# Experts' second matrix read by TensorE where it lies, through a register, instead of from a copy

## The chip, the cores and the metric

The kernel runs on one core of one Trainium2 chip. The metric is the device time of one execution in microseconds; the median of several runs counts. All data are float32 (indices are integers). The engines are TensorE (PE in the profile), VectorE (DVE), ScalarE (ACT), GpSimd (POOL) and SyncE (SP, which issues most of the transfers). Each works through its own program, and semaphores tie them together.

## The reference

x has 16 rows of 256 tokens of 128 numbers. Four blocks are added to it one after the other: a linear attention, a mixture-of-experts block, a second attention, and the same mixture-of-experts block again. The part that matters here is inside the block that runs twice:

```
logits = xf @ Wg.T
idx = jnp.argmax(logits, axis=-1)
for e in range(E):
    m = (idx == e)[:, None].astype(xf.dtype)
    h = jax.nn.relu(xf @ W1[e] + b1[e])
    out = out + m * (h @ W2[e] + b2[e])
z = _layer_norm(y + _moe(y, Wg, W1, b1, W2, b2), g2, be2)
```

There are 8 experts, W1[e] is 128x512 and W2[e] is 512x128. Each token goes through one expert.

## The kernel before

The 4096 tokens lie in DRAM sorted by expert, each expert's rows padded to whole tiles of 128. There are at most `ET` = 39 tiles, and a table `owner`, built by DVE in `table` shortly before, says for each tile which expert owns it. `experts(n, target)` runs for n = 0 and n = 1, once per mixture block; the two are called the two expert stages. All weights of the experts lie in SBUF for the whole kernel, in `we`: for each expert 512 columns of W1, then 512 of W2 and 128 more that carry the second bias and the residual (`EW` = 1152 columns). The scratch tile `late`, in three slots, is `we_t` in this stage.

Per tile i the engines do this:

- SP loads the tile's rows into `zs` (line 1238, one of nine slots).
- PE transposes them into the bank TB (1250). ACT copies the result to `zt` (1285, semaphore `zt`).
- ACT reads the tile's owner with a value load (1292) and copies the first matrix of that expert, 512 columns, from `we` to `we_t` (1293, semaphore `w1`). DVE reads the owner too (1305) and copies the other 640 columns (1334, semaphore `w2`).
- PE forms the hidden layer in four products (1260). The first two finish `hid_a`, which ACT turns into `hid_e` with a relu (1288, `relu_a`); the last two finish `hid_b`, DVE's share of the relu (1312, `relu_b`).
- PE forms the output in five products, four from `hid_e` (1271) and one from `zt` (1273), in one of three banks (`v`).
- DVE takes the statistics (1308, 1315, 1322), POOL the root (`rstd`, 1219), DVE finishes the layer norm (1318, 1329), and POOL writes the rows to their tokens in DRAM with an indirect transfer (1223).

A float32 product of 128x128 by 128x128 runs in two passes, each with its own weight load (PEld in the profile), so line 1260 has 8 passes per tile and lines 1271 and 1273 have 10.

The order on each engine is written out by hand. Every engine has a function `body(i, s, has, lap)` that holds step i of a software pipeline: `has(k)` says that the part that works on tile i - k is in it. `pipeline` (45) writes the first `first` steps out one by one, puts the rest into a loop of `unroll` steps, and writes the last steps out. PE and DVE have 12 steps written out and a loop of nine that runs three times, ACT has six and a loop of three. In PE's step i the order is: the transpose of tile i, the hidden layer of tile i - 1, the output of tile i - 2. In ACT's: `zt` of tile i, relu of tile i - 1, then owner and first matrix of tile i. In DVE's: owner of tile i, statistics of i - 3, relu of i - 1, the rest of the norm, and at the end the copy for tile i:

```
if has(0):
    after(dve, g["v"], o + i - 2)
    nc.vector.tensor_copy(we_t[:, c, F:], we[:, bass.ds(e, 1), F:].rearrange("p a n -> p (a n)"))\
        .then_inc(g["w2"], 1)
```

PE waits for `w1` ahead of line 1260 and for `w2` ahead of line 1271.
Of the kernel before, what the change touches and what calls it, by code (L numbers as in the profile page):

```python
# [29 lines left out]
P = 128  # L30
# [3 lines left out]
NT = T // P  # L34
# [4 lines left out]
F = 512  # L39
FC = F // P  # L40
E = 8
ET = (T + E * (P - 1)) // P
EW = F + F + D
# [29 lines left out]
def after(eng, sem, count):  # L73

    if not (isinstance(count, int) and count <= 0):
        eng.wait_ge(sem, count)

def build(nc, A, out):

    ctx = ExitStack()
    with ctx:
# [58 lines left out]
        we = sb("we", [P, E, EW])  # L141
# [7 lines left out]
        stats = sb("stats", [P, 3, 6, 6])  # L149
# [7 lines left out]
        zt = sb("zt", [P, 3, 2, 2 * P])  # L157
# [23 lines left out]
        owner = sb("owner", [P, ET], I32)  # L181
# [10 lines left out]
        late = sb("late", [P, 6144])  # L192
# [4 lines left out]
        def parts(whole, *shapes):  # L197

            at, cut = 0, []
            for shape in shapes:  # L200
                size = int(np.prod(shape))
                part = whole[:, at:at + size]
                names = "abcdef"[:len(shape)]
                if len(shape) > 1:
                    part = part.rearrange(f"p ({' '.join(names)}) -> p {' '.join(names)}",
                                          **dict(zip(names[1:], shape[1:])))
                cut.append(part)
                at += size
            assert at <= whole.shape[1], at
            return cut  # L210
# [15 lines left out]

        k_x, p_t = parts(early, (3, 2, 4, HM, 32), (3, 2, HM, P))

        we_t, over, owner_m, skip_m, ends_m = parts(late, (3, EW), (E, NT), (ET, E), (ET, E), (E, E))
        pay, zs = parts(rows_e, (3, 2, PAY), (ZS, PAY))  # L230
        hid_e, = parts(hid_f, (3, FC, P))

# [892 lines left out]
        def table(n):  # L1125
# [61 lines left out]

        e_s = {k: sem("e_" + k) for k in (
            "turned", "zt", "w1", "w2", "hid_a", "hid_b", "relu_a", "relu_b", "v", "stats", "agg", "var",  # L1190
            "rstd", "tmp", "dest", "y")}
        loaded = [sem(f"e_loaded{k}") for k in range(ZS)]
        stored = [sem(f"e_stored{k}") for k in range(3)]
# [5 lines left out]
        def experts(n, target):  # L1199

            o = n * ET
# [39 lines left out]
            def _(pe):  # L1242
                g = e_s

                def body(i, s, has, lap):
# [5 lines left out]
                    if has(1):  # L1251
# [11 lines left out]
                                last.then_inc(g["hid_a"], 1)  # L1263
                        last.then_inc(g["hid_b"], 1)
                    if has(2):
                        pe.wait_ge(g["relu_a"], o + i - 1)
                        pe.wait_ge(g["relu_b"], o + i - 1)
                        pe.wait_ge(g["w2"], o + i - 1)
                        after(pe, g["tmp"], o + i - 4)
                        for m in range(FC):  # L1270
                            nc.tensor.matmul(VB[c2][:, 0:P], hid_e[:, c2, m, :], we_t[:, c2, F + m * P:F + (m + 1) * P],  # L1271
                                             start=(m == 0), stop=False)
                        nc.tensor.matmul(VB[c2][:, 0:P], zt[:, c2, 0, 0:P], we_t[:, c2, 2 * F:], start=False,
                                         stop=True).then_inc(g["v"], 1)
                pipeline(pe, ET, 3, ZS, body, FIRST)

            @on("scalar")
# [21 lines left out]
            def _(dve):  # L1299
                g = e_s  # L1300

                def body(i, s, has, lap):
                    c, c1 = s % 3, (s - 1) % 3
                    if has(0):
                        e = dve.value_load(owner[0:1, bass.ds(i, 1)], min_val=0, max_val=E - 1)
                    if has(3):
                        dve.wait_ge(g["v"], o + i - 2)
                        nc.vector.bn_stats(stats[:, c, 0, :], VB[c][:, 0:P]).then_inc(g["stats"], 1)
# [14 lines left out]
                    if has(4):  # L1323
                        dve.wait_ge(g["tmp"], o + i - 3)
                        if has(7):
# [3 lines left out]
                        nc.vector.scalar_tensor_tensor(out=xout[:, c1, 0, :], in0=tmp[:, c1, 0, :],  # L1329
                                                       scalar=rstd[:, c1, 0:1], in1=row[:, D:2 * D], op0=ALU.mult,  # L1330
                                                       op1=ALU.add).then_inc(g["y"], 1)
                    if has(0):
                        after(dve, g["v"], o + i - 2)
                        nc.vector.tensor_copy(we_t[:, c, F:], we[:, bass.ds(e, 1), F:].rearrange("p a n -> p (a n)"))\
                            .then_inc(g["w2"], 1)
                dve.wait_ge(tabled, n * 2 + 1)
                pipeline(dve, ET, 5, ZS, body, FIRST)

# [226 lines left out]
```

## Time and profile before

| | |
|---|---|
| Median of 3 runs | 846.76 us (845.48 to 848.72) |
| The profiled execution: its own time | 845.9 us |
| The profiled execution: span of its instructions | 844.0 us |
| Mean granted clock of TensorE | 0.908 of full speed |
| Busy: PE, weight loads | 687.7 us (81%), 579.5 us (69%) |
| Busy: DVE, ACT, POOL | 547.8 us (65%), 338.1 us (40%), 476.0 us (56%) |

Busy time counts work on the engine; register operations, waits and the issue of transfers are not in it. The profile's span runs from the first to the last instruction; the execution's own time has 1.9 us more around it. The expert stages lie at about 336 to 436 us and at about 741 us to the end. In the rows further down, "ACT late L1293" is ACT's instruction of line 1293 that writes the tile `late`; a q behind an engine's name (ACTq, DVEq, and PEldq for PE) stands for that engine's sequencer.

### The profile page before, as it was taken

The page shows a single profiled execution, that of the slowest core. Times are in us where ns is not written, and L with a number is a line of the kernel's source. Part 1 is how long each engine was busy: PE and PEld are TensorE (multiplying, and loading weights), DVE is VectorE, ACT ScalarE, POOL GpSimd, SP SyncE. Part 2 cuts the span into 40 slices and gives each one's busy share as a digit, 9 for nine tenths or more (in the row PEclk, how much of TensorE's full clock was granted, in tenths as well). Part 3 has the DMA queues.
Part 4 walks back from the last instruction along what each step waited for, and adds up shares of the span by engine and source line. Part 5 has one row for each costly group of instructions (what it writes and reads, how often), then busy time and mean ns, then how long its engine had stood idle before and what let it go on. Part 6 is the DMA issues. An engine that isn't in the chain of part 4 may idle for free.

```text
span 844.0 us, 18577 instructions
## 1 busy us (share of the span) xinstructions
PE 687.7 (81%) x5238; PEld 579.5 (69%) x5238; DVE 547.8 (65%) x1972; ACT 338.1 (40%) x839; POOL 476.0 (56%) x1098
## 2 busy tenths in 40 slices
PE   5799999877888754999969999995788876089994
PEld 3588888734666653999955877774566755079994
DVE  3788887556999854688842333323489985248885
ACT  2332323125777510555532121220677762045552
POOL 5465656643688870388764233322348887127886
PEclk9999999979999857899988999998799995579997
DMA  7900000040011134233230000004001111423320
GB/s 225 291 13 15 12 19 13 26 106 2 13 39 37 45 126 87 73 86 93 72 108 18 20 13 19 19 14 118 1 2 38 46 42 45 82 73 87 93 84 31
DMA packets 54887, 49.50 MB, mean 59 GB/s; under 512 B 5768, under 2 KB 49743, under 8 KB 54704
## 3 DMA queue, kind: packets, MB, share of 16 engines
q1 hardware_dynamic: 46426, 33.51, 14.8%
q0 software_dynamic: 5568, 13.54, 4.5%
q10 hardware_dynamic: 2838, 1.78, 1.1%
q8 instruction: 26, 0.43, 0.2%
q14 instruction: 29, 0.24, 0.1%
HBM read 31.07 MB, written 19.85 MB: 60 GB/s over the span
## 4 chain that ended last, share of the span: by engine, by line
PE 45%; DVE 23%; POOL 9%; issue 8%; DMA 6%; ACT 4%; DVEq 1%; SPq 1%; ACTq 1%; POOLq 1%
PE bank L1260 7%; PE wide L1397 7%; PE bank L1386 7%; PE wide L1271 4%; DVE early L1029 4%; DVE early L736 3%; POOL rstd L534 3%; DVE stats L511 2%; PE bank L1271 2%; PE wide L456 2%; DVE z L538 2%; DMA sorted_dram<-sorted_dram 2%; POOL sorted_dram L1114 1%; PE wide L871 1%; DMA sorted_dram<-rows_e,pos 1%
## 5 line engine op out<-in xcount | busy, mean ns | idle before, releaser
L520 POOL TENSOR_TENSOR both_m<-stats 128x2 f32<-128x2 f32 (+1 forms) x94 | 19.1, 203 | 175.1 <-DVE stats L511 174.7
L1219 POOL TENSOR_TENSOR rstd<-var_e,half_neg 128x1 f32<-128x1 f32 x78 | 59.0, 756 | 84.3 <-DVE var_e L1322 79.4
L1260 PE MATMUL bank<-zt,late 128*128 128x128 f32 x624 | 90.9, 291 | 1.6 <-issue 1.2
L534 POOL TENSOR_TENSOR rstd<-spread_m,half_neg 128x2 f32<-128x2 f32 (+1 forms) x94 | 86.0, 915 | 7.4
L1260 PEld LDWEIGHTS bank<-zt,late 128*128 128x128 f32 x624 | 78.8, 198 | 8.3 <-issue 4.0
L1114 POOL DMA_INDIRECT sorted_dram<-rows_e,pos x64 | 66.7, 1043 | 15.5 <-issue 14.7
L1312 DVE TENSOR_SCALAR hid_f<-bank 128x256 f32<-128x256 f32 x78 | 33.1, 425 | 49.6 <-PE bank L1260 44.9
L1386 PE MATMUL bank<-late,qk_t 128*128 128x128 f32 x512 | 62.1, 275 | 0.0
L1293 ACT ACTIVATE late<-we 128x512 f32 x78 | 49.2, 631 | 28.6 <-PE bank L1260 24.4
L1397 PE MATMUL wide<-vo,gram 128*128 128x512 f32 x128 | 60.0, 612 | 0.7 <-ACT gram L1444 0.7
L1386 PEld LDWEIGHTS bank<-late,qk_t 128*128 128x128 f32 x512 | 59.6, 192 | 0.0
L1029 DVE STREAM_TRANSPOSE early<-sc 32x256 f32<-32x256 f32 x128 | 55.8, 436 | 1.5
L1271 PE MATMUL wide<-late,hid_f 128*128 128x128 f32 x416 | 55.1, 275 | 0.0
L1464 DVE COPY late<-wide 128x1024 f32<-128x1024 f32 x16 | 19.6, 1225 | 48.0 <-PE wide L1397 48.0
L1271 PEld LDWEIGHTS wide<-late,hid_f 128*128 128x128 f32 x416 | 50.6, 192 | 0.1
L1285 ACT ACTIVATE zt<-bank 128x128 f32<-128x128 f32 x78 | 21.6, 276 | 72.7 <-PE bank L1250 72.7
L1250 PE MATMUL bank<-ident,rows_e 128*128 128x128 f32 x78 | 22.4, 287 | 34.4 <-DMA rows_e<-sorted_dram 34.4
L959 ACT ACTIVATE early<-bank 32x256 f32<-32x256 f32 x128 | 47.4, 371 | 1.1
L1223 POOL DMA_INDIRECT out<-xout,dest x39 | 40.3, 1033 | 6.0 <-issue 5.5
L1223 POOL DMA_INDIRECT x_dram<-xout,dest x39 | 40.3, 1034 | 5.2 <-issue 4.8
L1397 PEld LDWEIGHTS wide<-vo,gram 128*128 128x128 f32 x128 | 23.9, 197 | 25.6 <-issue 24.3
L1288 ACT ACTIVATE hid_f<-bank 128x256 f32<-128x256 f32 x78 | 29.9, 383 | 25.5 <-PE bank L1260 25.5
(247 smaller groups left out, 1878.9 us busy)
## 6 DMA issues: line engine op xcount, KB each, us to landing
rows_e<-sorted_dram SPq DMA_DIRECT2D x78, 128.5 KB
xa<-x_dram SPq DMA_DIRECT2D x9, 640.0 KB, 6.4
we<-L_ffn_W SPq DMA_DIRECT2D x16, 256.0 KB
x_dram<-xout SPq DMA_DIRECT2D x32, 128.0 KB, 1.8
rows_e<-L_ffn_b SPq DMA_DIRECT2D x1, 2048.0 KB
xa<-L_attn_a_x SPq DMA_DIRECT2D x3, 512.0 KB, 6.1
sorted_dram<-sorted_dram ACTq DMA_DIRECT2D x8, 128.5 KB, 6.4
sorted_dram<-sorted_dram SPq DMA_DIRECT2D x8, 128.5 KB, 6.8
```

Source lines behind the costliest of these rows:

```text
L534: nc.gpsimd.tensor_tensor(rstd[:, slot, w], spread_m[:, slot, 0, w], half_neg[:, w], ALU.pow).then_inc(rstd_made, 1)
L959: last = nc.scalar.activation(k_x[rows, c1, :, :, h, :].rearrange("p t q k -> p (t q) k"), QK[rows, 256:512].rearrange("p (n k) -> p n k", ...
L1029: last = nc.vector.transpose(p_t[rows, c3, :, :, 32 * q:32 * q + 32].rearrange("p t h k -> p (t h) k"), sc[rows, c3, :, :, :].rearrange("p ...
L1114: nc.gpsimd.indirect_dma_start(sorted_dram[n][:, :], bass.IndirectOffsetOnAxis(ap=pos[:, c, t:t + 1], axis=0), pay[:, c, t, :], None).then ...
L1219: nc.gpsimd.tensor_tensor(rstd[:, s % 3, 0:1], var_e[:, s % 3, :], half_neg[:, 0:1], ALU.pow).then_inc(g["rstd"], 1)
L1223: nc.gpsimd.indirect_dma_start(target, bass.IndirectOffsetOnAxis(ap=dest[:, c, :], axis=0), xout[:, c, 0, :], None).then_inc(stored[(s - 5 ...
L1260: last = nc.tensor.matmul(to[:, (m % 2) * P:(m % 2 + 1) * P], we_t[:, c1, m * P:(m + 1) * P], zt[:, c1, 0, 0:P], start=True, stop=True)
L1271: nc.tensor.matmul(VB[c2][:, 0:P], hid_e[:, c2, m, :], we_t[:, c2, F + m * P:F + (m + 1) * P], start=(m == 0), stop=False)
L1293: nc.scalar.activation(we_t[:, c, 0:F], we[:, bass.ds(e, 1), 0:F].rearrange("p a n -> p (a n)"), ACT.Copy).then_inc(g["w1"], 1)
L1312: nc.vector.tensor_scalar_max(hid_e[:, c1, 2:4, :], HB_[:, 0:256].rearrange("p (m t) -> p m t", m=2), 0.0).then_inc(g["relu_b"], 1)
L1386: last = nc.tensor.matmul(MB[:, 0:P], qk_t[:, h, :], u_sb[:, c, h * D:(h + 1) * D], start=(h == 0), stop=(h == HB - 1))
L1397: last = nc.tensor.matmul(wide[:, 512 * k:512 * (k + 1)], gram[:, c2, :], vo[:, 4 * k:4 * k + 4, :].rearrange("p h d -> p (h d)"), start=T ...
```

## The change

DVE no longer reads the owner and no longer copies the second matrix; the semaphore `w2` and PE's wait for it are gone. `we_t` shrinks to the 512 columns of the first matrix. PE reads the owner of tile i - 2 itself, behind line 1260 and ahead of the output's products, and these take their second operand from `we` at an address from a register. DVE's wait for the table at the start of the stage moves to PE. ACT's part stays.

```diff
--- before.py
+++ after.py
@@ -226,7 +226,7 @@
 
         k_x, p_t = parts(early, (3, 2, 4, HM, 32), (3, 2, HM, P))
 
-        we_t, over, owner_m, skip_m, ends_m = parts(late, (3, EW), (E, NT), (ET, E), (ET, E), (E, E))
+        we_t, over, owner_m, skip_m, ends_m = parts(late, (3, F), (E, NT), (ET, E), (ET, E), (E, E))
         pay, zs = parts(rows_e, (3, 2, PAY), (ZS, PAY))
         hid_e, = parts(hid_f, (3, FC, P))
 
@@ -1187,7 +1187,7 @@
 
 
         e_s = {k: sem("e_" + k) for k in (
-            "turned", "zt", "w1", "w2", "hid_a", "hid_b", "relu_a", "relu_b", "v", "stats", "agg", "var",
+            "turned", "zt", "w1", "hid_a", "hid_b", "relu_a", "relu_b", "v", "stats", "agg", "var",
             "rstd", "tmp", "dest", "y")}
         loaded = [sem(f"e_loaded{k}") for k in range(ZS)]
         stored = [sem(f"e_stored{k}") for k in range(3)]
@@ -1263,15 +1263,17 @@
                                 last.then_inc(g["hid_a"], 1)
                         last.then_inc(g["hid_b"], 1)
                     if has(2):
+                        e = pe.value_load(owner[0:1, bass.ds(i - 2, 1)], min_val=0, max_val=E - 1)
+                        second = we[:, bass.ds(e, 1), F:].rearrange("p a n -> p (a n)")
                         pe.wait_ge(g["relu_a"], o + i - 1)
                         pe.wait_ge(g["relu_b"], o + i - 1)
-                        pe.wait_ge(g["w2"], o + i - 1)
                         after(pe, g["tmp"], o + i - 4)
                         for m in range(FC):
-                            nc.tensor.matmul(VB[c2][:, 0:P], hid_e[:, c2, m, :], we_t[:, c2, F + m * P:F + (m + 1) * P],
+                            nc.tensor.matmul(VB[c2][:, 0:P], hid_e[:, c2, m, :], second[:, m * P:(m + 1) * P],
                                              start=(m == 0), stop=False)
-                        nc.tensor.matmul(VB[c2][:, 0:P], zt[:, c2, 0, 0:P], we_t[:, c2, 2 * F:], start=False,
+                        nc.tensor.matmul(VB[c2][:, 0:P], zt[:, c2, 0, 0:P], second[:, F:], start=False,
                                          stop=True).then_inc(g["v"], 1)
+                pe.wait_ge(tabled, n * 2 + 1)
                 pipeline(pe, ET, 3, ZS, body, FIRST)
 
             @on("scalar")
@@ -1301,8 +1303,6 @@
 
                 def body(i, s, has, lap):
                     c, c1 = s % 3, (s - 1) % 3
-                    if has(0):
-                        e = dve.value_load(owner[0:1, bass.ds(i, 1)], min_val=0, max_val=E - 1)
                     if has(3):
                         dve.wait_ge(g["v"], o + i - 2)
                         nc.vector.bn_stats(stats[:, c, 0, :], VB[c][:, 0:P]).then_inc(g["stats"], 1)
@@ -1329,11 +1329,6 @@
                         nc.vector.scalar_tensor_tensor(out=xout[:, c1, 0, :], in0=tmp[:, c1, 0, :],
                                                        scalar=rstd[:, c1, 0:1], in1=row[:, D:2 * D], op0=ALU.mult,
                                                        op1=ALU.add).then_inc(g["y"], 1)
-                    if has(0):
-                        after(dve, g["v"], o + i - 2)
-                        nc.vector.tensor_copy(we_t[:, c, F:], we[:, bass.ds(e, 1), F:].rearrange("p a n -> p (a n)"))\
-                            .then_inc(g["w2"], 1)
-                dve.wait_ge(tabled, n * 2 + 1)
                 pipeline(dve, ET, 5, ZS, body, FIRST)
```

Two places show the change in the order of instructions. The first is PE, a tile inside the loop; the names are the tiles and banks written and read, and the semaphores waited for stand in brackets. Before:

```order
L1260 MATMUL bank<-zt,late 128x128 [waits e_relu_a,e_w1,e_zt]
L1260 MATMUL bank<-zt,late 128x128
L1260 MATMUL bank<-zt,late 128x128 [waits e_relu_b]
L1260 MATMUL bank<-zt,late 128x128
L76 REGISTER_ALU [waits e_w2,e_relu_b,e_relu_a]
L1271 MATMUL bank<-late,hid_f 128x128 [waits e_tmp]
L1271 MATMUL bank<-late,hid_f 128x128 x3
L1273 MATMUL bank<-late,zt 128x128
L76 REGISTER_ALU [waits e_loaded6]
```

And now (line 1266 is the value load, 1272 and 1274 are the former 1271 and 1273):

```order
L1260 MATMUL bank<-zt,late 128x128 [waits e_relu_a,e_w1,e_zt]
L1260 MATMUL bank<-zt,late 128x128
L1260 MATMUL bank<-zt,late 128x128 [waits e_relu_b]
L1260 MATMUL bank<-zt,late 128x128
L1266 ISA
L1266 TENSOR_LOAD owner
L1266 ISA x2
L1272 ISA [waits e_tmp,e_relu_b,e_relu_a]
L1272 MATMUL wide<-we,hid_f 128x128
L1272 ISA
L1272 MATMUL wide<-we,hid_f 128x128
L1272 ISA
```

A load and three register operations stand between line 1260 and the output's first product, and one register operation (ISA) ahead of each of the products, of which the last two follow in the same way. Of the three waits of L76, that for `e_w2` is gone.

The second place is DVE, one tile of the loop, before:

```order
L1305 TENSOR_LOAD owner
L1305 ISA x2
L1308 BN_STATS stats<-wide 128x6 [waits e_v]
L1312 TENSOR_SCALAR hid_f<-bank 128x256 [waits e_hid_b,e_stats]
L1315 BN_AGGR mv<-stats 128x2
L1318 SCALAR_TENSOR_TENSOR tmp<-bank,mv,g2f 128x128 [waits e_rstd]
L1322 TENSOR_SCALAR var_e<-mv 128x1 [waits e_agg]
L1328 COPY dest<-rows_e 128x1 [waits e_stored0,e_tmp]
L1329 SCALAR_TENSOR_TENSOR xout<-tmp,rstd,rows_e 128x128
L1334 ISA [waits e_v]
L1334 COPY late<-we 128x640
```

And now:

```order
L1308 BN_STATS stats<-wide 128x6 [waits e_v]
L1312 TENSOR_SCALAR hid_f<-bank 128x256 [waits e_hid_b,e_stats]
L1315 BN_AGGR mv<-stats 128x2
L1318 SCALAR_TENSOR_TENSOR tmp<-wide,mv,g2f 128x128 [waits e_rstd]
L1322 TENSOR_SCALAR var_e<-mv 128x1 [waits e_agg]
L1328 COPY dest<-rows_e 128x1 [waits e_stored1,e_tmp]
L1329 SCALAR_TENSOR_TENSOR xout<-tmp,rstd,rows_e 128x128
```

The load at the head and the copy at the end are gone; the seven instructions between them keep their order and their waits.

## Rows read from the trace of the kernel before

**Rows 1.** The page, the chain that ended last: shares of the span by line.

```profile
PE bank L1260 7%; PE wide L1397 7%; PE bank L1386 7%; PE wide L1271 4%; DVE early L1029 4%; DVE early L736 3%; POOL rstd L534 3%; DVE stats L511 2%; PE bank L1271 2%; PE wide L456 2%; DVE z L538 2%; DMA sorted_dram<-sorted_dram 2%; POOL sorted_dram L1114 1%; PE wide L871 1%; DMA sorted_dram<-rows_e,pos 1%
```

**Rows 2.** Windows over tiles 6 to 37 of the first expert stage.

```profile
core 0: us, PE busy (x) PEld busy (x) DVE busy (x) ACT busy (x) POOL busy (x), PEclk, DMA share, GB/s
352.90:424.00 71.10, 71.10 (x609) 68.63 (x607) 61.01 (x256) 41.32 (x96) 56.76 (x64) 1.00 0.30 84
```

**Rows 3.** The chain in order of time: start us, us, engine and line, passes.

```profile
344.56 0.89 PE bank L1260 x8
...
346.68 0.89 PE bank L1260 x8
...
353.04 1.01 PE bank L1260 x8
...
357.51 0.94 PE bank L1260 x8
...
359.68 1.01 PE bank L1260 x8
...
424.15 1.05 PE bank L1260 x8
```

**Rows 4.** Timeline, loop tiles: start us, us, engine line operation out<-in, count, [idle before].

```profile
380.32 0.38 ACT L1288 ACTIVATE hid_f<-bank 128x256 f32<-128x256 f32 x1 [0.28 <-PE bank L1260]
...
381.10 0.63 ACT L1293 ACTIVATE late<-we 128x512 f32 x1 [0.39 <-PE bank L1260]
...
381.80 0.97 PEld L1260 LDWEIGHTS bank<-zt,late 128*128 128x128 f32 x8
...
382.55 0.38 ACT L1288 ACTIVATE hid_f<-bank 128x256 f32<-128x256 f32 x1 [0.28 <-PE bank L1260]
382.68 0.97 PEld L1271 LDWEIGHTS bank<-late,hid_f 128*128 128x128 f32 x8
...
383.11 0.42 DVE L1312 TENSOR_SCALAR hid_f<-bank 128x256 f32<-128x256 f32 x1
383.26 0.63 ACT L1293 ACTIVATE late<-we 128x512 f32 x1 [0.33 <-issue]
```

**Rows 5.** PE's sequencer (PEldq) in narrow windows: duration ns min/median/max, first and last start.

```profile
L76 PEldq EVENT_SEMAPHORE  x1: 1029/1029/1029, 380.7 to 380.7; - x1
...
L1268 PEldq EVENT_SEMAPHORE  x1: 51/51/51, 381.8 to 381.8; - x1
...
L76 PEldq EVENT_SEMAPHORE  x1: 51/51/51, 381.9 to 381.9; - x1
...
L65 PEldq ALU_OP  x1: 32/32/32, 382.1 to 382.1; - x1
```

**Rows 6.** Waits of the first stage's steady part: total us, times, longest.

```profile
ACT late L1293 <- PE bank L1260: 10.7, 28, 0.4
POOL rstd L1219 <- DVE var_e L1322: 10.0, 27, 0.6
```

**Rows 7.** DVE's value load (L1305, both stages) and copy (L1334, first stage), by source line.

```profile
L1305 DVEq FUSED_REGOPS  x126: 57/190/206, 326.4 to 828.5; - x126
L1305 DVEq TENSOR_LOAD <-owner x78: 299/306/554, 325.8 to 828.1; - x78
...
L1334 DVE COPY late<-we x32: 483/485/495, 353.0 to 422.1; 128x640 f32 x32
```

**Rows 8.** ACT's value load and copy of one tile, by source line.

```profile
L1292 ACTq FUSED_REGOPS  x2: 43/98/152, 380.4 to 380.8; - x2
L1292 ACTq TENSOR_LOAD <-owner x1: 275/275/275, 380.5 to 380.5; - x1
L1292 ACTq SEQ_ASSERT  x1: 18/18/18, 381.0 to 381.0; - x1
...
L1293 ACTq FUSED_REGOPS  x1: 46/46/46, 381.0 to 381.0; - x1
```

**Rows 9.** The page, DMA queues: packets, MB, share of 16 engines.

```profile
q8 instruction: 26, 0.43, 0.2%
```

## The prediction

> **What bounds the kernel now.** I began with the page's chain that ended last: L1260, the experts' first product, stands at its head with 7%, and L1271, the second, is near it [rows 1]. The change lies in the two expert stages, so next came the windows over their steady part (tiles 6 to 37): PE is busy in every microsecond of it, DVE 61 of 71 us, ACT 41, and the granted clock is 1.00, which is the 2.4 GHz level [rows 2]. A full PE looks like a PE bound. The chain in order of time corrects that: in the first tiles L1260 comes every 2.12 us and takes 0.89, from 353 on it comes every 2.16 to 2.24 us (357.51 to 359.68 is one tile, 353.04 to 357.51 are two) and is stretched to 0.93 to 1.01, with the same eight passes [rows 3]. From 353.04 to 424.15 there are 32 tiles, 2.22 us each. So PE loses about 0.1 us in each of 33 tiles per stage, just ahead of L1260, which the page hides in its busy time.
>
> The timeline of one tile shows for what. ACT's copy of the first matrix (L1293) runs from 381.10 to 381.73, and L1260 loads its first weights at 381.80 [rows 4]; PE's sequencer sat in the wait of that moment for 1029 ns from 380.7 [rows 5]. In the next tile the copy ends at 383.89. Thus the bound is a ring: L1260 starts (381.80), its first half gives relu_a on ACT (382.55), ACT reads the owner and forms the address, copies (383.26 to 383.89), and L1260 may start again. **DVE is not in that ring.** The waits of the stretch hold none of PE for DVE's w2: the longest are POOL for DVE's var_e and ACT for L1260 [rows 6].
>
> **The change part by part.** *Taken from DVE:* 78 copies of 128x640 at 485 ns (38 us) and 78 value loads, in which the sequencer spends 306 + 190 ns and more [rows 7]. Who profits? PE asked for w2 two tiles late, so not PE. stats (L1308) could start up to 0.5 us earlier, since it stands behind the copy of 0.49, but bn_aggr, var and POOL's rstd come after relu_b (383.11), which waits for L1260 [rows 4, 6]. I cost the relief at 0; what hides it is that relu_b is tied to PE. If POOL were the last (57 of 71 us busy [rows 2]) it would gain at most those few tenths at a stage's end, once per stage. The wait for w2 falls from PE too; its operation of 51 ns stays in part, since two waits remain.
>
> *Added on PE:* per tile a TENSOR_LOAD, a register operation behind it and an assert, in loop tiles one more register operation for the table's address, and five register operations, one ahead of each of the five products (ten passes). None is array work, all of it is the sequencer's. It does run ahead of the array: it was at the loop's end (L65, 382.1) while L1260's passes of 381.80 to 382.68 were still running, ahead of all of L1271 [rows 4, 5]. But it can't run ahead over the wait for w1, which holds it until 381.77. After that the array is fed until L1271's slot at 382.68, so there are 0.91 us in which the new operations must be through. What do they need? The same value load on ACT takes 43 (address) + 275 + 152 + 18 ns, and 46 more for the copy's address, from 380.4 to the copy's start at 381.10: 0.70 us, so some 30 ns lie between two of them [rows 4, 8]. On PE two operations of 51 ns start at 381.84 and 381.95 (rows from windows of 0.02 us) and the next at 382.1, a good 0.1 apart, so the gaps there are nearer 58 ns [rows 5]. From the gate: 0.075 until the first operation (381.77 to 381.84), 0.101 + 0.336 + 0.210 + 0.076 for the load, 0.109 for the remaining wait, 0.096 for the first address: 1.00 us. In tiles that also form a wait's count (two of the loop's nine) 0.09 more, 1.09. In tiles written out without the loop the table's address falls away: 0.90, in time.
>
> So in the 54 loop tiles L1272 starts 0.09 late, in 12 of these 0.18. PE's own work is 2.12, so it is ready after 2.21 or 2.30, while the ring allows 2.16, 2.23 or 2.24 in turn [rows 3]. Most of the lateness falls into time that PE lost to the ring anyway. I followed it tile by tile: L1272 starts at the later of S + 0.89 and gate + 1.00 (1.09), PE is ready 1.23 later, the next S is the later of that and the ring's; a late S gives the sequencer a lead over the array that shortens the next lateness. 27 tiles come out 0.46 us longer, both stages **+0.9 us**.
>
> Bounds of the two unknown prices. The load: at ACT's 275 ns as above; DVE's median of 306 gives +1.4, and 0.41 us, between that and DVE's worst (554), would give +3.8; a cheaper one than ACT's could save no more than the 0.9 [rows 7, 8]. The register-addressed product: no row of PE has one. Low end: static products, of which the sequencer passes 20 instructions between its wait at 381.9 and the operation at 382.1, next to nothing. High end: each of two passes costs a slot like PE's cheapest operation, 32 + 60 ns, 0.184 per product [rows 5]. The nearest row is ACT's register-addressed copy, which starts at 381.10, directly behind its address operation of 46 ns at 381.0 [rows 4, 8]; I take that, a few hundredths. PE then needs some 0.12 to 0.2 of its sequencer per product, below the array's 0.22 for two passes, and nothing is added; the loss begins at 0.10 extra per product.
>
> The Trainium skill speaks against the change here: "TensorE: Matmul & The Clock Gate", section "Wait — 56ns, not 53.3ns?", says that MATMUL is normally decoded in hardware, and that the sequencer's own code, where it has to do it, spends about 62 ns on each. If a register in the address forces that, by an estimate from this figure the extra is 0.124 per product, the sequencer needs 2.33 us per tile, and the sum would be +6.4 instead of +0.9, 853 us. The trace agrees with hardware decoding for static products (20 in 0.1 us); no row here shows the other.
>
> The head and the tail: the first two tiles are cold and have over 1.6 us between L1260 and L1271; the last product waits for its predecessor, not for its sequencer. 0. **Sum:** 844.0 + 0.9 in the span, with the 1.9 around it 846.8 for the profiled execution. That one ran 0.9 below the median of the runs, 846.76, so I forecast a median of **847.7 us**.
>
> **The rivals.**
> 1. *The sequencer becomes the bound (slower).* Price: from the gate 1.00 + four products' operations 0.50 + the extra + 0.19 for the next tile's wait and transpose + 0.03. It decides from an extra of about 0.10 per product. At the high end (5 x 0.184) that is 2.64 per tile, +0.4 in 54 loop tiles and +0.3 in 18 others, about +28, 875 us; halfway between decision and high end some +14, 861. For it: each operation of PE's sequencer has its 0.1 us, and nothing shows a register-addressed pass there. Against it: ACT's copy. 22%.
> 2. *The load waits for PE's passes to end (slower).* L1260's last pass ends 1.05 after S, the load and what follows take 0.83, so L1272 starts at 1.88 instead of 0.89, +0.9 in 78 tiles: 917 us. Against it: ACT's load begins at 380.5 while its relu_a runs (380.32 to 380.70) [rows 4, 8]. 4%.
> 3. *The loop's code no longer stays in the engine (slower).* PE's loop of nine tiles grows from some 380 instructions (38 passes and weight loads a tile, and some four others) by eight a tile to some 455. A packet of code takes 0.2% of 16 x 844 us over 26 packets, 1.0 us [rows 9]; two of them exposed at each of four back edges is +8, 856 us. 26 packets for the whole run speak against. 3%.
> 4. *The ring isn't the bound and PE is delayed by DVE after all (faster).* Then the 66 tiles fall from 2.22 to 2.12: 66 x 0.10 = -6.8, 840 us. Against it: 0.07 us from the copy's end to L1260 in tile after tile. 5%.
> That the change does less than it says is no case: in the order of instructions the copy and DVE's load are gone, and PE has its own.
>
> **How the numbers follow.** Forecast 66%, from 844.5 to 851 us (load at 0.41, spread of the median). Runs of this kernel tell 0.5% (4.2 us) from no change. Slower: 22 + 4 + 3%, less the mild part of rival 1, plus little of the forecast's own upper end: 29%. Faster: 6%. Within: 65%. The range reaches down to 844.5, which leaves out the 5% of rival 4, and up to 858, which takes in the mild half of rival 1 and rival 3, and leaves out about 15%.
>
> **What would show it.** Right: L1293's end to L1260's start still 0.07 in most tiles, pitch of the loop tiles 2.22 to 2.25, idle or stretch of up to 0.1 ahead of L1272, DVE some 50 us less busy and more idle, POOL unchanged. Rival 1: a pitch of 2.3 or more, L1293 done long before L1260, a stretched L1272. Rival 2: a gap of 1 us ahead of L1272. Rival 3: a gap at the loop's ends alone, and more code packets. Rival 4: 2.12. I am wrong if PE's operations have another price than ACT's.

## The result, and the profile after

| | Before | Changed |
|---|---|---|
| Median, 20 runs each | 847.12 us (844.72 to 850.09) | 848.91 us (846.54 to 852.62) |
| Changed over before | | 1.0026, 95% interval 1.0015 to 1.0037 |
| Profiled execution: own time, span | 845.9 us, 844.0 us | 852.62 us, 850.9 us |

By the ratio the changed kernel takes 2.2 us more of 847 (1.3 to 3.1). It is slower, by less than the 0.5% that the prediction called a difference. The forecast was "within 0.5%", +0.9 us.

The profiled execution of the changed kernel is the slowest of its 20, so its span may not be compared with [rows 1]'s run as a whole. 2.1 us of the 6.9 between the two spans had passed before the first expert product was issued (340.03 against 337.93), where the kernels are the same; 1.5 more lie in the first six tiles of the first stage, which the section on the prediction comes to. The page:

```profile
PE 692.5 (81%) x5238; PEld 585.3 (69%) x5239; DVE 514.2 (60%) x1893; ACT 338.5 (40%) x839; POOL 470.7 (55%) x1098
...
q8 instruction: 28, 0.46, 0.3%
...
PE bank L1260 9%; PE wide L1392 7%; PE bank L1381 7%; PE wide L1272 6%; DVE early L1029 4%; PE bank L1272 3%; DVE early L736 3%; DVE stats L511 2%; POOL rstd L534 2%; DVE z L538 2%; DMA sorted_dram<-sorted_dram 2%; ACT z L974 2%; PE wide L456 2%; DVE sc L1020 1%; DMA sorted_dram<-rows_e,pos 1%
...
L1219 POOL TENSOR_TENSOR rstd<-var_e,half_neg 128x1 f32<-128x1 f32 x78 | 51.1, 655 | 90.5 <-DVE var_e L1322 85.8
...
L1312 DVE TENSOR_SCALAR hid_f<-bank 128x256 f32<-128x256 f32 x78 | 33.1, 425 | 92.6 <-PE bank L1260 59.9
```

DVE lost 33.6 us of busy time (547.8 before), and not a microsecond of it shows in the span: ahead of L1312 it now sits idle for 92.6 us (49.6 before), most of it until PE's L1260 is done. The chain names the same two products as [rows 1], with larger shares. Code packets are 28 instead of 26 [rows 9].

The windows over the 32 tiles from tile 6 to tile 38, first and second expert stage, answer to [rows 2]:

```profile
core 0: us, PE busy (x) PEld busy (x) DVE busy (x) ACT busy (x) POOL busy (x), PEclk, DMA share, GB/s
356.52:429.01 72.49, 72.47 (x609) 70.24 (x608) 47.02 (x225) 41.37 (x96) 54.29 (x65) 1.00 0.29 82
763.70:836.64 72.94, 72.74 (x609) 70.09 (x607) 46.79 (x225) 41.37 (x96) 54.15 (x65) 1.00 0.29 82
```

For the second stage of the kernel before, the same view gives:

```profile
758.53:829.83 71.30, 71.30 (x609) 68.62 (x607) 60.88 (x254) 41.31 (x96) 56.94 (x64) 1.00 0.29 84
```

The first number after the bounds is the length; over 32 it is the pitch of a tile. It was 2.22 us in the first stage and 2.23 in the second, and is 2.27 and 2.28 now, at the same passes and the same granted clock of 1.00. That is +3.0 us over 2 x 32 tiles in this pair of executions, against +2.2 in the timed runs. DVE falls from 61 to 47 us of work in the stretch, ACT stays at 41. PE reads busy throughout in all of these rows, so the busy column tells nothing of the loss. What tells it is the timeline, at the place of [rows 4]:

```profile
380.69 0.63 ACT L1295 ACTIVATE late<-we 128x512 f32 x1 [0.33 <-PE bank L1260]
...
381.47 0.97 PEld L1260 LDWEIGHTS bank<-zt,late 128*128 128x128 f32 x8
...
382.22 0.38 ACT L1290 ACTIVATE hid_f<-bank 128x256 f32<-128x256 f32 x1 [0.17 <-PE bank L1260]
...
382.41 0.97 PEld L1272 LDWEIGHTS wide<-we,hid_f 128*128 128x128 f32 x8
...
383.70 0.97 PEld L1260 LDWEIGHTS bank<-zt,late 128*128 128x128 f32 x8
...
384.87 0.30 PEld L1272 LDWEIGHTS wide<-we,hid_f 128*128 128x128 f32 x2 [0.20 <-issue]
```

Before, L1271 followed L1260 by 0.89 us in every tile. L1272 now follows by 0.94 (381.47 to 382.41) and by 1.17 (383.70 to 384.87), the latter with 0.20 us of empty weight path, released by nobody ("issue"). Over tiles 6 to 38 the mean of this distance is 1.01 us. PE's sequencer shows why, in the first of the two tiles: narrow windows on the wait, the load, the remaining wait and the first address (a q view rounds starts to 0.1):

```profile
L76 PEldq EVENT_SEMAPHORE  x1: 357/357/357, 381.0 to 381.0; - x1
...
L1266 PEldq FUSED_REGOPS  x2: 42/96/151, 381.4 to 381.9; - x2
L1266 PEldq TENSOR_LOAD <-owner x1: 307/307/307, 381.5 to 381.5; - x1
L1266 PEldq SEQ_ASSERT  x1: 18/18/18, 382.1 to 382.1; - x1
...
L76 PEldq EVENT_SEMAPHORE  x1: 51/51/51, 382.2 to 382.2; - x1
...
L1272 PEldq FUSED_REGOPS  x1: 60/60/60, 382.3 to 382.3; - x1
```

The wait for w1 ends at 381.37, 0.05 after ACT's copy (380.69 + 0.63). Then come six operations one after the other, and only at 382.41 the weight load of L1272: 1.04 us after the gate, where 1.00 was forecast. The load is the difference. Over the stretch of the first window its row reads:

```profile
L1266 PEldq FUSED_REGOPS  x59: 42/151/151, 356.9 to 427.4; - x59
L1266 PEldq TENSOR_LOAD <-owner x32: 298/306/417, 356.6 to 427.0; - x32
```

and in the six tiles of it that are written out ahead of the loop:

```profile
L1266 PEldq TENSOR_LOAD <-owner x6: 301/366/417, 356.6 to 368.0; - x6
```

It takes 306 ns in the median, like DVE's, and not 275 like ACT's [rows 7, 8]; the mean over both stages is 317, and nine of the 78 took over 340.

### The profile page after: what moved, and what is told of

It is laid out like the page before. It is cut to its first block, busy times and chain, and to the rows that moved or that the text cites. A ratio compares the mean times of both kernels' runs of the same rounds, so it can differ in the third digit from the quotient of the medians.

```text
span 850.9 us, 18752 instructions
## 1 busy us (share of the span) xinstructions
PE 692.5 (81%) x5238; PEld 585.3 (69%) x5239; DVE 514.2 (60%) x1893; ACT 338.5 (40%) x839; POOL 470.7 (55%) x1098
## 4 chain that ended last, share of the span: by engine, by line
PE 50%; DVE 22%; issue 8%; POOL 7%; DMA 6%; ACT 5%; SPq 1%; ACTq 1%; POOLq 0%; DVEq 0%
PE bank L1260 9%; PE wide L1392 7%; PE bank L1381 7%; PE wide L1272 6%; DVE early L1029 4%; PE bank L1272 3%; DVE early L736 3%; DVE stats L511 2%; POOL rstd L534 2%; DVE z L538 2%; DMA sorted_dram<-sorted_dram 2%; ACT z L974 2%; PE wide L456 2%; DVE sc L1020 1%; DMA sorted_dram<-rows_e,pos 1%
## 5 line engine op out<-in xcount | busy, mean ns | idle before, releaser
L1219 POOL TENSOR_TENSOR rstd<-var_e,half_neg 128x1 f32<-128x1 f32 x78 | 51.1, 655 | 90.5 <-DVE var_e L1322 85.8
L1260 PE MATMUL bank<-zt,late 128*128 128x128 f32 x624 | 89.0, 288 | 1.7 <-issue 1.3
L1312 DVE TENSOR_SCALAR hid_f<-bank 128x256 f32<-128x256 f32 x78 | 33.1, 425 | 92.6 <-PE bank L1260 59.9
L1260 PEld LDWEIGHTS bank<-zt,late 128*128 128x128 f32 x624 | 79.9, 200 | 4.4 <-issue 3.0
L1295 ACT ACTIVATE late<-we 128x512 f32 x78 | 49.2, 631 | 28.4 <-issue 18.5
L1272 PE MATMUL wide<-we,hid_f 128*128 x416 | 58.5, 284 | 0.1
L1272 PEld LDWEIGHTS wide<-we,hid_f 128*128 128x128 f32 x416 | 50.5, 192 | 3.0 <-issue 1.1
L918 PE MATMUL wide<-early,v_r 128*32 128x128 f32 x512 | 22.3, 296 | 21.1 <-DVE early L1029 21.1
```

The source lines that it names most:

```text
L1219: nc.gpsimd.tensor_tensor(rstd[:, s % 3, 0:1], var_e[:, s % 3, :], half_neg[:, 0:1], ALU.pow).then_inc(g["rstd"], 1)
L1260: last = nc.tensor.matmul(to[:, (m % 2) * P:(m % 2 + 1) * P], we_t[:, c1, m * P:(m + 1) * P], zt[:, c1, 0, 0:P], start=True, stop=True)
L1272: nc.tensor.matmul(VB[c2][:, 0:P], hid_e[:, c2, m, :], second[:, m * P:(m + 1) * P], start=(m == 0), stop=False)
L1295: nc.scalar.activation(we_t[:, c, 0:F], we[:, bass.ds(e, 1), 0:F].rearrange("p a n -> p (a n)"), ACT.Copy).then_inc(g["w1"], 1)
L1312: nc.vector.tensor_scalar_max(hid_e[:, c1, 2:4, :], HB_[:, 0:256].rearrange("p (m t) -> p m t", m=2), 0.0).then_inc(g["relu_b"], 1)
```

## The experiments

All are compared with the kernel before on the same chip. "Pitch" is the length of tiles 6 to 38 over 32, first and second stage. "Distance" is the mean time from the first weight load of the hidden layer (L1260) to that of the output (L1271, L1272), and "gate" the median time from the end of ACT's copy to L1260; both are read from the starts and ends in the timeline of the first stage.

| Run | Ratio to before (95%) | Pitch, us | Distance | Gate |
|---|---|---|---|---|
| before | 1 | 2.223, 2.228 | 0.888 | 0.07 |
| changed | 1.0026 (1.0015 to 1.0037) | 2.265, 2.280 | 1.013 | 0.11 |
| e1_early_load | 1.0001 (0.9987 to 1.0014) | 2.230, 2.229 | 0.888 | 0.07 |
| e2_load_only | 1.0013 (0.9998 to 1.0027) | 2.256, 2.263 | 1.006 | 0.08 |
| e3_two_loads | 1.0297 (1.0270 to 1.0325) | 2.608, 2.614 | 1.378 | 0.42 |
| e4_before_act_swap | 0.9950 (0.9932 to 0.9968) | 2.179, 2.189 | 0.952 | 0.40 |
| e5_after_act_swap | 0.9955 (0.9942 to 0.9968) | 2.209, 2.219 | 0.976 | 0.50 |
| e6_early_act_swap | 0.9899 (0.9880 to 0.9918) | 2.142, 2.136 | 0.890 | 0.40 |
| e7_relief_alone | 0.9986 (0.9972 to 1.0000) | 2.223, 2.226 | 0.888 | 0.07 |
| e9_three_loads | 1.0888 (1.0825 to 1.0952) | 3.192, 3.243 | 1.963 | 1.00 |

**Is it the load's place?** e1_early_load is the changed kernel with one edit: PE's load and the address stand at the head of its step, ahead of the transpose and of the wait for w1.

```diff
                     c, c1, c2 = s % 3, (s - 1) % 3, (s - 2) % 3
+                    if has(2):
+                        e = pe.value_load(owner[0:1, bass.ds(i - 2, 1)], min_val=0, max_val=E - 1)
+                        second = we[:, bass.ds(e, 1), F:].rearrange("p a n -> p (a n)")
                     if has(0):
...
                     if has(2):
-                        e = pe.value_load(owner[0:1, bass.ds(i - 2, 1)], min_val=0, max_val=E - 1)
-                        second = we[:, bass.ds(e, 1), F:].rearrange("p a n -> p (a n)")
                         pe.wait_ge(g["relu_a"], o + i - 1)
```

> The changed kernel with PE's value load moved from behind L1260 to the head of the step, ahead of the transpose and of the wait for w1, where PE's sequencer has time to spare. All register addresses and register-addressed products stay. Theory (the load and what follows stand between the w1 gate and the output's first product): the distance from L1260's start to the output's first product falls from 0.95 to 1.1 back to 0.89, the pitch of the gated tiles from 2.27 back to 2.22, and the time to that of the kernel before, 847 us within 1. Rival (the register-addressed products, the longer code, or something outside the expert stages makes the change slower): the time stays 2 us above before, pitch 2.27.

Its time is that of the kernel before, 844.95 against 844.96 us. The windows of both stages:

```profile
354.20:425.57 71.37, 71.35 (x609) 68.78 (x607) 45.54 (x225) 41.30 (x96) 54.39 (x65) 1.00 0.29 83
758.24:829.58 71.34, 71.34 (x609) 68.79 (x608) 45.58 (x225) 41.30 (x96) 54.25 (x65) 1.00 0.28 83
```

71.37 and 71.34 stand beside 71.15 and 71.30 before: all but 0.3 of the 3.0 us is gone, though every added instruction is still there. Ahead of the gate the load runs while PE's sequencer would wait anyway. The other additions, the ten register-addressed passes, the grown loop and its two more code packets, thus cost little. How little is told by e7 further down, which has the same relief of DVE and none of the additions: against it e1's steady tiles are 0.4 us longer in all, and its time 1.3 us by the two ratios, which is no more than their intervals leave open.

**The load without the rest.** e2_load_only is the kernel before, with the load behind L1260; DVE's copies stay and only the fifth product reads through the register. It has the load but neither the relief nor the other four addresses.

```diff
                     if has(2):
+                        e = pe.value_load(owner[0:1, bass.ds(i - 2, 1)], min_val=0, max_val=E - 1)
+                        second = we[:, bass.ds(e, 1), F:].rearrange("p a n -> p (a n)")
                         pe.wait_ge(g["relu_a"], o + i - 1)
...
-                        nc.tensor.matmul(VB[c2][:, 0:P], zt[:, c2, 0, 0:P], we_t[:, c2, 2 * F:], start=False,
+                        nc.tensor.matmul(VB[c2][:, 0:P], zt[:, c2, 0, 0:P], second[:, F:], start=False,
```

> The kernel before with PE's value load added behind L1260 and used for one product alone, the last of the five; DVE still copies the second matrix and the other four products read the copy. Theory: the load alone carries the cost, L1260 to the output's first product becomes 0.95 to 1.1, pitch 2.25 to 2.28, +2 to +3 us against before (849 to 850). Rival (the cost lies in the register-addressed products, or DVE's relief hides a larger one): with four of five gone the cost is under 0.5 us, pitch 2.22; or, if DVE's relief had helped, more than +4.

Measured is +1.1 us with an interval that just reaches zero, less than expected. The profile is clearer than the time: the distance is 1.006 and the pitch 2.256 and 2.263, some two thirds (second stage) to four fifths (first) of what the changed kernel adds. So the load alone makes most of the loss of the steady tiles; by time it makes half (1.1 of 2.2), with intervals too wide to tell the rest's share.

**The relief without the load.** e7_relief_alone takes DVE's load and copy away and gives PE a fixed address, so it leaves out the choice of the second matrix: seven experts of eight get the wrong one.

```diff
-                        pe.wait_ge(g["w2"], o + i - 1)
...
-                            nc.tensor.matmul(VB[c2][:, 0:P], hid_e[:, c2, m, :], we_t[:, c2, F + m * P:F + (m + 1) * P],
+                            nc.tensor.matmul(VB[c2][:, 0:P], hid_e[:, c2, m, :], we[:, 0, F + m * P:F + (m + 1) * P],
...
-                        e = dve.value_load(owner[0:1, bass.ds(i, 1)], min_val=0, max_val=E - 1)
...
-                        nc.vector.tensor_copy(we_t[:, c, F:], we[:, bass.ds(e, 1), F:].rearrange("p a n -> p (a n)"))\
-                            .then_inc(g["w2"], 1)
```

> The kernel before without DVE's owner load and without its copy of the second matrix, and nothing in their place: PE takes the second matrix of expert 0 for every tile, from its fixed address, so the output's second product is left with the wrong matrix for seven experts of eight. It shows DVE's relief alone. Theory (DVE is in no ring of the kernel before): the same time as before within 1 us, pitch 2.22, DVE some 40 us less busy. Rival (the relief gives something that the change's costs ate up): 2 us or more below before.

```profile
353.25:424.37 71.12, 71.12 (x609) 68.63 (x607) 45.56 (x225) 41.30 (x96) 54.38 (x65) 1.00 0.29 84
756.43:827.65 71.22, 71.22 (x609) 68.63 (x607) 45.59 (x225) 41.29 (x96) 54.34 (x65) 1.00 0.29 83
```

DVE has 15 us less to do in each stretch, and the stretch keeps its length to 0.1 us. The ratio leaves between 0 and 2.4 us in all, which then lie outside the steady tiles; where, I did not find.

**Is the ring the bound?** e4_before_act_swap is the kernel before with ACT's order changed: owner and first matrix of tile i come ahead of the relu of tile i - 1, so that the copy no longer waits for L1260 to fill `hid_a`.

```diff
-                    if has(1):
-                        act.wait_ge(g["hid_a"], o + i)
-                        nc.scalar.activation(hid_e[:, c1, 0:2, :], HA_[:, 0:256].rearrange("p (m t) -> p m t", m=2),
-                                             ACT.Relu).then_inc(g["relu_a"], 1)
                     if has(0):
                         after(act, g["hid_b"], o + i - 2)
                         e = act.value_load(owner[0:1, bass.ds(i, 1)], min_val=0, max_val=E - 1)
                         nc.scalar.activation(we_t[:, c, 0:F], we[:, bass.ds(e, 1), 0:F].rearrange("p a n -> p (a n)"),
                                              ACT.Copy).then_inc(g["w1"], 1)
+                    if has(1):
+                        act.wait_ge(g["hid_a"], o + i)
...
```

> The kernel before with one thing changed: in each of ACT's steps the owner's load and the copy of the first matrix come ahead of relu_a of the tile before, so that the copy no longer waits for L1260's first half. Theory (the ring L1260, relu_a, load, copy, L1260 sets the pitch of tiles 6 to 38): the pitch falls from 2.22 to PE's own 2.12, 66 tiles, -6 to -7 us, 840 to 841. Rival (PE or DVE sets the pitch itself and the 0.07 between copy and L1260 is a coincidence): the time stays 847, or rises where relu_a becomes late.

It gains 4.2 us by the ratio, where 6 to 7 were expected. The gate opens early (0.40 instead of 0.07 from the copy's end to L1260), and the six steady tiles written out ahead of the loop fall to 2.12 and 2.13, PE's own work. So the ring was the bound. The loop tiles stop at 2.19 and 2.20 in the mean; most take 2.12 too, and a few much longer. Now PE does wait for DVE at times, which no row of the kernel before showed; the waits of 350 to 425 us:

```profile
DVE stats L1308 <- issue: 3.4, 11, 0.6
DVE dest L1328 <- DMA x_dram<-xout,dest: 1.8, 3, 1.3
PEld bank L1260 <- DVE hid_f L1312: 1.3, 3, 0.8
```

With the ring loosened, DVE's work has a price. Part of it is slack: the longest of PE's three waits, 0.8 us, goes back to a store whose landing DVE awaited for 1.3 us ahead of L1328, and that tile took 2.95 us. In e6 further down DVE has the same wait of 1.3 us, and no steady tile takes more than 2.40. So this is where the change should pay.

**The same swap on the changed kernel**, e5_after_act_swap:

> The changed kernel (PE's load behind L1260) with ACT's load and copy put ahead of relu_a, as in the run before last. With the ring gone PE's sequencer passes the wait for w1 early and has about 1.75 us of operations per tile against 2.12 of the array, and DVE has no copy and no load. Theory (the change's load costs only where the sequencer is held at the w1 gate, and DVE's work, which held the swapped kernel before at 2.18 to 2.19, is now lighter): pitch 2.12 to 2.13, 6.5 to 7 us below before, 838 to 839, 3 us better than the same swap without the change. Rival (PE's load costs wherever it stands): pitch 2.17 or more, no better than the swap alone.

It missed the 2.12: 2.209 and 2.219, no better than e4. What explains it is the row of the load over tiles 6 to 38 of the first stage, where its median is 331 ns instead of 306, and the timeline of one tile:

```profile
L1266 PEldq TENSOR_LOAD <-owner x33: 297/331/482, 351.5 to 422.2; - x33
```

```profile
396.65 0.63 ACT L1291 ACTIVATE late<-we 128x512 f32 x1 [0.50 <-issue]
...
397.19 0.36 ACT L1295 ACTIVATE hid_f<-bank 128x256 f32<-128x256 f32 x1
...
397.74 0.97 PEld L1260 LDWEIGHTS bank<-zt,late 128*128 128x128 f32 x8
...
398.76 0.41 PEld L1272 LDWEIGHTS wide<-we,hid_f 128*128 128x128 f32 x3
```

The copy (L1291) is done at 397.28, long before L1260, but the same wait also asks for relu_a, which now comes last on ACT (L1295 ends at 397.55). The gate has only changed its owner, the load still stands behind it, and L1272 follows L1260 by 1.02 us. Without the ring to hide in, the lateness is paid whole: 2.12 + (0.976 - 0.888) = 2.21, which is the pitch.

**Both edits**, e6_early_act_swap (e1 with ACT's new order):

> The same with PE's load at the head of the step as well. Theory: nothing is left for the early place to hide, the same time as the run without it within 0.5 us, pitch 2.12. Rival (the load behind L1260 still delays the products): 1 to 3 us faster than that run.

```profile
350.34:418.89 68.55, 68.55 (x610) 68.11 (x608) 45.63 (x225) 37.72 (x96) 53.94 (x64) 1.00 0.30 87
749.67:818.03 68.36, 68.36 (x610) 67.98 (x608) 45.60 (x225) 37.73 (x96) 54.05 (x64) 1.00 0.29 87
```

It beats both kernels: 835.08 against 843.85 us for the kernel before in the same call, 8.5 us by the ratio (6.9 to 10.1). The pitch is 2.14, within 0.02 of PE's own work. I had expected it to equal e5. It is 4.9 us faster (839.98 to 835.08), and the pitches account for that: (2.209 - 2.142 + 2.219 - 2.136) x 33 = 5.0 us. Against e4, which has the same swap with DVE's copies, the steady tiles are 3 us shorter by the pitches (0.8 of it is e4's one tile of 2.95); here the relief of DVE is worth something at last.

**How does the cost grow?** e3_two_loads adds a second load of the same number behind the gate, used for the fifth product:

```diff
+                        e2 = pe.value_load(owner[0:1, bass.ds(i - 2, 1)], min_val=0, max_val=E - 1)
                         e = pe.value_load(owner[0:1, bass.ds(i - 2, 1)], min_val=0, max_val=E - 1)
...
-                        nc.tensor.matmul(VB[c2][:, 0:P], zt[:, c2, 0, 0:P], second[:, F:], start=False,
+                        nc.tensor.matmul(VB[c2][:, 0:P], zt[:, c2, 0, 0:P], we[:, bass.ds(e2, 1), 2 * F:].rearrange("p a n -> p (a n)"), start=False,
```

> The changed kernel with a second value load of the same number directly behind the first, used for the fifth product. It adds about 0.1 for the address, 0.36 and 0.21 for the load and its register operations and 0.08 for the assert, 0.75 us between the gate and the output's first product. Theory: L1260 to the output's first product about 1.65 to 1.75, PE ready 1.23 later, pitch about 2.95 in the loop tiles and 2.85 in the others, 45 to 52 us above before (892 to 899). Rival (the sequencer's time lies beside the array's and costs little): twice the change's loss, +4 us, 851.

```profile
353.01:436.45 83.44, 76.36 (x609) 70.26 (x608) 48.16 (x225) 41.29 (x96) 54.50 (x65) 1.00 0.24 70
```

It costs 25 us, half of what I expected: a load with what follows it takes 0.65 us of the sequencer, and the pitch grows by 0.34 (2.27 to 2.61). My sum had charged 0.65 us per tile against a gate that opens when L1260 could start. But a late output makes the next L1260 late, while ACT's copy is timed by the L1260 before. So the gate opens x earlier than L1260 starts, and the sequencer uses x for its load. Two equations fix x. By the ring the copy ends 2.22 - 0.07 = 2.15 after L1260, so the pitch is 2.15 + x. By PE it is 2.12 plus the lateness, and L1272 (here L1273) comes 1.80 after the copy's end (0.42 + 1.38, e3's own reading), so this is 2.12 + 1.80 - x - 0.89. Then x = 0.44 and the pitch 2.59; measured are 0.42 and 2.61. Since the 1.80 is taken from the same run, this shows that the two equations close, not that they forecast. By them every further microsecond behind the gate would be paid half.

e9_three_loads adds a third, to test that:

```diff
+                        e2 = pe.value_load(owner[0:1, bass.ds(i - 2, 1)], min_val=0, max_val=E - 1)
+                        e3 = pe.value_load(owner[0:1, bass.ds(i - 2, 1)], min_val=0, max_val=E - 1)
                         e = pe.value_load(owner[0:1, bass.ds(i - 2, 1)], min_val=0, max_val=E - 1)
```

> The changed kernel with a third value load behind L1260, each used for products. A load with its register operation and assert took 0.66 us of PE's sequencer in the run with two. First theory (the whole lateness is paid): pitch 2.61 + 0.66 = 3.27, 45 us and more above the run with two loads, 915 or more. Second theory, formed after that run (half is paid: a late L1260 starts the ring later, so the sequencer passes the next w1 gate earlier relative to the array; pitch = (time from the copy's end to the output's first product + 1.23 + 2.14) / 2): pitch 2.61 + 0.33 = 2.94, L1260 starts 0.75 after the copy, +21 to +24 us over the run with two loads, 890 to 894.

The half rule gave 890 to 894 and fails: 920.21 us. The size of the whole rule comes out, and not its reason. One tile of its sequencer, narrow windows on the three loads and the next wait:

```profile
L1266 PEldq TENSOR_LOAD <-owner x2: 302/304/306, 402.8 to 405.9; - x2
...
L1267 PEldq TENSOR_LOAD <-owner x1: 304/304/304, 403.4 to 403.4; - x1
...
L1268 PEldq TENSOR_LOAD <-owner x1: 300/300/300, 404.1 to 404.1; - x1
```

```profile
L76 PEldq ALU_OP  x1: 32/32/32, 405.6 to 405.6; - x1
L76 PEldq EVENT_SEMAPHORE  x1: 51/51/51, 405.7 to 405.7; - x1
```

```profile
404.17 0.63 ACT L1297 ACTIVATE late<-we 128x512 f32 x1 [0.41 <-PE bank L1260]
...
405.01 0.97 PEld L1274 LDWEIGHTS wide<-we,hid_f 128*128 128x128 f32 x8 [1.41 <-issue]
```

The copy ends at 404.80, and PE's sequencer comes to its wait only at 405.70, right behind its last operation; in 29 of 33 tiles no more than 0.14 us lies between that operation's end and the wait's (10 of 33 in e3, 1 of 33 in the changed kernel). One tile is the sequencer's own chain, 402.76 to 405.93 = 3.17 us (starts from windows of 0.02 us), of which the three loads with what follows them take 0.65 each; 1.22 is left for everything else. With one load that chain is 1.87 us and with two 2.52, both under their pitch. So there are three regimes: hidden ahead of the gate (e1), paid half behind it (e3), and paid nearly whole once the sequencer itself is the bound (e9, 0.58 and 0.63 of 0.65 in the pitch).

## Why the prediction was right, and where it was off

- **"The bound is a ring", right.** e4 loosens only that ring, and the written-out tiles go to the 2.12 that was named as PE's own work; they had been 2.24.
- **"DVE is not in that ring", relief at 0: right for this kernel.** e7 shows an unchanged pitch, and the time leaves 2.4 us at most. It would have been wrong with the ring loosened (e4 against e6).
- **The place of the cost, right.** Load and addresses "can't run ahead over the wait for w1". e1 moves only this and gets all of it back.
- **+0.9 us, too small: +2.2 (1.3 to 3.1).** The failing step is the term "The load: at ACT's 275 ns". PE's load took 306, for which the prediction's own other end said +1.4, and 317 in the mean. On the line between that end and +3.8 at 0.41 us, a load of 317 makes some +1.6. Step by step from the gate to L1272 the tile shown has 1.04 against the sum's 1.00, and 0.03 of the difference is the load.
- **"In tiles written out without the loop ... 0.90, in time": wrong.** Their loads took 366 ns in the median of six, and their pitch rose from 2.238 to 2.272 in the first stage and from 2.239 to 2.290 in the second, +0.5 us over 12 tiles. With the +1.6 that is 2.1, near the measured 2.2, and in part by luck: in the same pair of executions the loop tiles' pitch rose from 2.220 to 2.264 and from 2.226 to 2.277, +2.5 us and not 1.6. Choosing the nearest row by kind (ACT's) rather than the dearer of two rows was the mistake; both rows were on the table [rows 7, 8].
- **The register-addressed product, "a few hundredths", nothing added: right.** In the tile shown the address operations take 46 ns and start 0.124 us apart with two passes between them, against the array's 0.22. Of the 0.124, the operation is 46 ns and the usual gap 58, so the two passes with their weight loads take 0.02.
- **Rival 1 (sequencer the bound), refuted at one load, reached at three.** Its conditions were a pitch of 2.3 and a gate left long open; here 2.27 and 2.28, and the wait for w1 is still a real one in 32 of 33 tiles. The 62 ns per MATMUL that the Trainium skill gives for the sequencer's own code ("TensorE: Matmul & The Clock Gate", section "Wait — 56ns, not 53.3ns?") would by an estimate have made 853 us; e1, with the same ten passes, is at the time of before, so no such cost shows.
- **Rival 2 (load waits for PE's passes), refuted.** The load starts at 381.55, while L1260's passes run until after 382.4. **Rival 3 (code), refuted**: 28 packets instead of 26, the same in e1, which costs nothing. **Rival 4 (DVE held PE), refuted** by e7.
- **The signs named for "right": half of them came.** DVE has more idle time, and L1272 is late. But the pitch of the loop tiles is 2.26 and 2.28, outside "2.22 to 2.25" and short of rival 1's 2.3; the gate's 0.07 became 0.11 and 0.10; L1272 is late by 0.12 us in the mean and by 0.28 at most, where 0.1 was named. "DVE some 50 us less busy" counted the value loads, which aren't in the busy time: it is 33.6. "POOL unchanged" missed rstd, 0.1 us shorter (last section).
- **Head and tail 0: the tail shown, the head hidden by the clock.** From the start of the second stage's tile 38 to the end it is 14.22 us before and 14.21 after. The first six tiles of the first stage took 1.5 us longer in the changed kernel's execution (16.49 against 14.97), those of the second 0.15. TensorE's granted clock accounts for it: it rose from half to full 5.8 us after the first L1260 before (at 343.7), and 8.9 us after it in the changed kernel (at 349.0). Half of the 3.2 us between them is 1.6. The windows around the two rises, before and changed (the granted clock is the third number from the end):

```profile
342.00:344.00 2.00, 2.00 (x13) 2.00 (x12) 0.83 (x2) 1.01 (x2) 0.00 (x0) 0.57 0.40 109
344.00:346.00 2.00, 2.00 (x21) 2.00 (x20) 0.73 (x3) 0.98 (x3) 0.00 (x0) 1.00 0.12 40
```

```profile
348.00:349.00 1.00, 1.00 (x6) 1.00 (x6) 0.00 (x0) 0.51 (x2) 0.00 (x0) 0.51 0.00 0
349.00:350.00 1.00, 1.00 (x11) 1.00 (x10) 0.67 (x3) 0.51 (x1) 0.04 (x1) 1.00 0.00 0
```

The rise comes 6.6 and 6.8 us after the first L1260 in the second stages of the two, and 7.5 and 6.8 us after it in the first stages of e1 and e7 (15.78 and 15.44 us for the six tiles). So it moves between executions, also with no load on PE (e7), and whether the change moves it isn't shown.

What stays open: why some loads on PE take 340 to 520 ns, and why they are rarer with the load ahead of the gate (one of 78 over 340 ns in e1, nine in the changed kernel, 31 in e5).

## What to carry to other kernels

A value load on an engine costs its sequencer, not its unit, and what it costs the kernel hangs on which wait it stands behind: 0.65 us of load and what follows was free ahead of PE's gate and cost 2.2 us in all behind it, moved by one edit of three lines. Taking work from an engine that is off the ring brought nothing that could be told from the noise until the ring was loosened; then the same relief paid some 3 us (e6 against e4), a part of the 8.5 us that e6 gains in all. So look for the order on the engine that closes the ring before moving work off its neighbours. When an instruction waits for several things, hastening the last to arrive can merely uncover the next (relu_a in e5).

## What the runs showed of the hardware

- A TENSOR_LOAD of one number from SBUF has its price by engine: in the median 278 to 279 ns on ACT, 272 to 275 on SP, 300 to 308 on PE (311 in e5) and 306 on DVE; the register operation behind it takes 151 to 152 ns on PE and ACT, 190 on DVE.
- A product whose operand is addressed through a register runs at the pace of a static one: passes 0.11 us apart in both (L1272 and L1271), one register operation per product, of 46 ns in the median of the changed kernel (46 to 66).
- POOL's rstd, the operation of L1219, took 655 ns in the mean instead of 756. The seven kernels without DVE's copy of 128x640 and its load have 649 to 663, the three with them 754 to 764. Its row in e7:

```profile
L1219 POOL TENSOR_TENSOR rstd<-var_e,half_neg 128x1 f32<-128x1 f32 x78 | 51.2, 657 | 83.4 <-DVE var_e L1319 79.3
```

Before, the copy ran beside it (382.06 to 382.55 beside 381.74 to 382.58 in one tile). In the kernel before, three of the 78 rstd ran beside a copy and beside no load, and took 713 to 736 ns; seven ran beside neither and took 566 to 634. That speaks for the copy and against DVE's load, but these few lie at the stages' ends, and no run tried the two apart. POOL wasn't the last, so the tenth of a microsecond was worth nothing either.
